# Differential attention with a feed-forward: row loads issued one pair earlier, values projected ahead of the maxima, and a reordered end

## The reference

```
q, k, v = x@Wq/2, x@Wk, x@Wv        # 32 query/key heads of width 4, 16 value heads of width 8
p       = softmax(causal(q k^T))    # for each of the 2*32 heads, 1024 x 1024
a       = (p[even heads] - lam * p[odd heads]) @ v     # lam from four small vectors
a       = a * rsqrt(mean(a^2) + eps) * rms_w * (1 - lambda_init)
x1      = layernorm(x + a @ Wo)
xr, xk  = mixes of x1 and x1 shifted by one token
out     = layernorm(x1 + sigmoid(xr@W_r^T) * (relu(xk@W_k^T)^2 @ W_v^T))
```

## Time and profile before

| | |
|---|---|
| median of 3 runs | 469.9 us (469.86 to 471.97) |
| profiled execution: its time, its span | 472.3 us, 470.6 us |
| busy: PE, DVE, ACT, POOL | 411.2, 400.3, 351.6, 224.7 us |
| mean granted clock of TensorE | 0.932 of 2.4 GHz |

### The profile page before, as it was taken

How to read it: one execution, slowest core, us unless ns; L and a number is a source line. 1 busy time by engine, 2 the same in 40 slices (tenths; PEclk the granted TensorE clock), 3 DMA queues, 4 the chain that set the end, 5 groups by cost and what they waited for, 6 DMA issues and landing times.

```text
span 470.6 us, 16533 instructions
## 1 busy us (share of the span) xinstructions
PE 411.2 (87%) x5697; PEld 193.0 (41%) x5697; DVE 400.3 (85%) x563; ACT 351.6 (75%) x734; POOL 224.7 (48%) x514
## 2 busy tenths in 40 slices
PE   5669998999998999999999999999899999999473
PEld 2235443444443443444444443444344444545352
DVE  1688898999999999999999999999999999675625
ACT  2511687888888888888888888888888888886143
POOL 7100122256554656555555555555555555557412
PEclk9855588999999999999999999999999999999777
DMA  5469311111111111111111111111111111000001
GB/s 141 166 221 329 105 48 47 48 47 49 47 49 45 45 45 45 45 45 45 45 45 45 45 45 45 45 45 45 45 45 45 45 47 47 26 3 2 22 24 45
DMA packets 21390, 28.44 MB, mean 60 GB/s; under 512 B 4960, under 2 KB 9952, under 8 KB 21232
## 3 DMA queue, kind: packets, MB, share of 16 engines
q1 hardware_dynamic: 20768, 27.58, 19.4%
q10 hardware_dynamic: 592, 0.46, 0.3%
HBM read 20.39 MB, written 9.47 MB: 63 GB/s over the span
## 4 chain that ended last, share of the span: by engine, by line
PE 36%; issue 15%; DMA 15%; DVE 12%; SPq 10%; ACT 10%; POOL 1%; ACTq 1%; DVEq 1%; POOLq 0%
DMA km<-k_rows 14%; PE acc L665 10%; PE mx L581 9%; ACT e_buf L1011 7%; DVE part_max L1112 7%; SPq L310 5%; PE ex L635 4%; SPq L296 3%; PE mx L590 2%; PE ex L692 1%; SPq L318 1%; DMA x_tok<-in_L_attn_x 1%; DVE turn_max L1125 1%; ACT max_rows L884 1%; PE mx L805 1%
## 5 line engine op out<-in xcount | busy, mean ns | idle before, releaser
L1112 DVE TENSOR_REDUCE part_max<-mx 128x2 f32<-128x1024 f32 (+2 forms) x288 | 340.5, 1214 | 27.1 <-PE mx L590 20.0
L1011 ACT ACTIVATE e_buf<-ex 128x512 f32<-128x512 f32 x576 | 304.8, 601 | 50.1 <-PE ex L635 44.7
L665 PE MATMUL acc<-e_buf,v_grp 128*32 128x256 f32 x2756 | 182.5, 354 | 7.4 <-POOL v_grp L447 2.6
L502 POOL TENSOR_SCALAR_AFFINE_SELECT e_buf<-e_buf 128x256 f32<-128x256 f32 x256 | 100.8, 412 | 166.7 <-ACT e_buf L1011 166.7
L635 PE MATMUL ex<-qe,ke 26*128 26x512 bf16 (+3 forms) x768 | 147.7, 335 | 0.7 <-ACT e_buf L1011 0.5
L581 PE MATMUL mx<-km,qm 29*128 29x128 bf16 (+3 forms) x1280 | 118.2, 272 | 19.9 <-DMA km<-k_rows 10.6
L581 PEld LDWEIGHTS mx<-km,qm 26*128 26x128 bf16 (+1 forms) x1280 | 42.3, 94 | 121.1 <-DVE part_max L1112 59.5
L665 PEld LDWEIGHTS acc<-e_buf,v_grp 128*32 128x32 f32 x2756 | 65.2, 109 | 61.7 <-issue 32.9
L635 PEld LDWEIGHTS ex<-qe,ke 26*128 26x128 bf16 x768 | 46.2, 91 | 22.4 <-ACT e_buf L1011 9.0
L485 POOL TENSOR_TENSOR r_rms<-sq_eps,minus_half 128x16 f32<-128x16 f32 x15 | 43.6, 2909 | 0.1
L590 PE MATMUL mx<-mask,pick 32*128 32x128 bf16 x512 | 26.7, 224 | 0.0
(11 more groups left out here) (137 smaller groups left out, 274.8 us busy)
## 6 DMA issues: line engine op xcount, KB each, us to landing
qm<-q_rows SPq DMA_DIRECT2D x32, 128.0 KB, 2.5
km<-k_rows SPq DMA_DIRECT2D x32, 128.0 KB, 2.6
qe<-q_rows SPq DMA_DIRECT2D x32, 128.0 KB, 2.6
ke<-k_rows SPq DMA_DIRECT2D x32, 128.0 KB, 2.7
q_rows<-part_q SPq DMA_DIRECT2D x6, 256.0 KB, 5.7
k_rows<-part_k SPq DMA_DIRECT2D x6, 256.0 KB, 5.3
q_rows<-part_q SPq DMA_DIRECT2D x6, 192.0 KB
k_rows<-part_k SPq DMA_DIRECT2D x6, 192.0 KB
```

The lines of the kernel that those rows point to most:

```text
L502: pool.affine_select(out=e, in_=e, compare_op=ALU.is_ge, fill=0.0, base=0, pattern=[[0, PAIR], [1, P]], channel_multiplier=-1)\
L665: last = pe.matmul(out, v, e, start=first, stop=over, skip_group_check=True)
L1011: nc.scalar.activation(e_buf[:, b, i, :], ex[:, ex_slot(b, i) % EX_BANKS, :], ACT.Exp).then_inc(s["exped"], 1)
L1112: nc.vector.tensor_reduce(target, mx_of(n, pr, m)[:].rearrange("p s (a b) -> p s a b", a=a), AX.X, ALU.max).then_inc(s["maxed"], 1)
```

## The change

It has four parts.

1. **SP's queue.** `load_max_rows` is issued for pair n+3 ahead of `place_maxima(n+1)`, and `load_exp_rows(n+2)` behind it. The opening loads the rows of pair 1 for the exponentials and of pair 2 for the maxima ahead of `place_maxima(0)`. The 12 writes of batch 1 go between the first pairs: 6 behind `pair(0)`, 4 behind `pair(1)`, 2 behind `pair(2)`. The fill rows of batch 1 go behind `place_maxima(0)`, and `rms_col` behind `pair(3)`.
2. **Values.** They are projected ahead of the first unit, into the `wide` banks (those of `mx`): chunks 0 and 1 after `turn_x(3)`, chunks 2 and 3 after the last q and k. DVE copies chunks 0 and 1, ACT chunks 2 and 3. Unit 0 waits for DVE's copies, unit 1 for ACT's. The body no longer waits for values.
3. **Opening, DVE and ACT.** `remainder(6)`, `low(5)`, `remainder(7)` move ahead of unit 0; `low(6)` and `low(7)` stand behind units 0 and 1. `turn_weights` moves from unit 13 to unit 4. The scaling of `wo` by the rms weights moves from the opening to the end of DVE's loop.
4. **End.** `norm_ffn` is cut into `gate_ffn` and the rest. `normalise_half(0)` goes ahead of `gate_ffn(1)`, `normalise_half(1)` and `place_half(0)` ahead of `norm_ffn(1)`, and `apply2(0)`, `apply2(1)` behind `norm_attn(3)`.

```diff
             write_parts(sp, 0, slice(HEAD, P), s["rows_b0"])
+            load_exp_rows(sp, 1, 1)
+            load_max_rows(sp, 2, 0)
+            place_maxima(sp, 0, 0, 0)
             fill_rows(1, s["rows_b1"])
-            write_parts(sp, 1, slice(0, P), s["rows_b1"])
-            sp.wait_ge(s["bounce_in"], 16)
-            sp.dma_start(rms_col[:], w_bounce.rearrange("h w -> (h w)").unsqueeze(1)).then_inc(s["rms_in"], 16)
-            place_maxima(sp, 0, 0, 0)
 
             def pair(n, pr, g):
+                if not isinstance(n, int) or n + 3 < NPAIR:
+                    load_max_rows(sp, n + 3, 1 - pr)
+                if not isinstance(n, int) or n + 1 < NPAIR:
+                    place_maxima(sp, n + 1, 1 - pr, g + pr)
                 if not isinstance(n, int) or n + 2 < NPAIR:
-                    load_max_rows(sp, n + 2, pr)
-                if not isinstance(n, int) or n + 1 < NPAIR:
-                    load_exp_rows(sp, n + 1, 1 - pr)
-                    place_maxima(sp, n + 1, 1 - pr, g + pr)
+                    load_exp_rows(sp, n + 2, pr)
...
-            group(0)
+            def write_second(part):
+                for w in range(2):
+                    write_part(sp, w, part, 1, slice(0, P), s["rows_b1"])
+
+            pair(0, 0, 0)
+            write_second(0)
             sp.wait_ge(s["rows_b0"], 16 * 2 * len(TERMS))
-            group(1)
+            pair(1, 1, 0)
+            write_second(1)
+            pair(2, 0, 1)
+            write_second(2)
+            pair(3, 1, 1)
+            sp.wait_ge(s["bounce_in"], 16)
+            sp.dma_start(rms_col[:], w_bounce.rearrange("h w -> (h w)").unsqueeze(1)).then_inc(s["rms_in"], 16)
...
-            pool.wait_ge(s["v_copied"], NCH)
+            pool.wait_ge(s["v_copied_d"], 2)
+            pool.wait_ge(s["v_copied_a"], 2)
...
-            def project_v(ch, i):
-                if i == 0:
-                    pe.wait_ge(s["wv_in"], 16)
-                    pe.wait_ge(s["rest_done"], 2 * NCH)
-                t = 4 * ch + i
-                valued = pe.matmul(narrow[ch][:, P * i:P * (i + 1)], xT[:, P * t:P * (t + 1)], wv_sb[:], start=True,
-                                   stop=True)
-                if i == 3:
-                    valued.then_inc(s["v_done"], 1)
+            def project_v(ch):
+                pe.wait_ge(s["wv_in"], 16)
+                for t in range(4 * ch, 4 * ch + 4):
+                    last = pe.matmul(wide[ch][:, P * (t % 4):P * (t % 4 + 1)], xT[:, P * t:P * (t + 1)], wv_sb[:],
+                                     start=True, stop=True)
+                last.then_inc(s["v_done"], 1)
...
             turn_x(3)
+            project_v(0)
+            project_v(1)
             for ch in (2, 3):
                 pe.wait_ge(s["xt_copied_d"], ch)
                 project_qk(2 * ch)
                 project_qk(2 * ch + 1)
+            project_v(2)
+            project_v(3)
+            pe.wait_ge(s["v_copied_d"], 2)
...
-            values = {3 + i: [(V_ORDER[i // 4], i % 4)] for i in range(12)}
-            values[NU + EARLY - 2] = [(V_ORDER[3], 0), (V_ORDER[3], 1)]
-            values[NU + EARLY - 1] = [(V_ORDER[3], 2), (V_ORDER[3], 3)]
             for u in range(NU + EARLY):
+                if u == 1:
+                    pe.wait_ge(s["v_copied_a"], 2)
                 max_unit(0, u // NU, u % NU)
-                for ch, i in values.get(u, []):
-                    project_v(ch, i)
+                if u == 4:
+                    pe.wait_ge(s["rest_done"], 2 * NCH)
+                    turn_weights()
                 if u == NU + 3:
                     turn_maxima(0, 2)
-                if u == NU + 4:
-                    turn_weights()
             pe.wait_ge(s["wt_scaled"], 1)
-            pe.wait_ge(s["v_copied"], NCH)
...
+            for ch in range(2):
+                dve.wait_ge(s["v_done"], ch + 1)
+                nc.vector.tensor_copy(value_place(ch), wide[ch].rearrange("p (k g w) -> p k g w", k=4, g=GPB))\
+                    .then_inc(s["v_copied_d"], 1)
...
+            remainder(6)
+            low(5)
+            remainder(7)
             dve.wait_ge(s["parts_set"], 3)
-            late = {0: [(remainder, 6), (low, 5)], 1: [(remainder, 7), (low, 6)], 2: [(low, 7)],
+            late = {0: [(low, 6)], 1: [(low, 7)],
                     NU: [(combine, 0, 0)], NU + 1: [(split_high, 0)], NU + 2: [(split_low, 0)]}
...
+            gate_ffn(0)
             norm_ffn(0)
             square_k(1)
-            norm_ffn(1)
             normalise_half(0)
-            apply2(0)
+            gate_ffn(1)
             normalise_half(1)
             place_half(0)
+            norm_ffn(1)
             place_half(1)
             norm_attn(2)
+            norm_attn(3)
+            apply2(0)
             apply2(1)
-            norm_attn(3)
```

More of the change, by code:

```diff
@@ L95 @@
 EX_BANKS = 3
-V_ORDER = (2, 3, 0, 1)
 def ex_slot(b, i):
@@ L896, in middle, with copy_values @@
                                rest[:, m % 4, :]).then_inc(s["mid_done"], 1)
-            def copy_values(i):
-                ch = V_ORDER[i]
-                b, kb = ch // 2, ch % 2 * 4
-                act.wait_ge(s["v_done"], i + 1)
-                src = narrow[ch].rearrange("p (k g w) -> p k g w", k=4, g=GPB)
-                dst = v_all[:].rearrange("p (b g k w) -> p b k g w", b=B, g=GPB, k=NB)[:, b, kb:kb + 4]
-                nc.scalar.copy(dst, src).then_inc(s["v_copied"], 1)
+            def copy_values(ch):
+                act.wait_ge(s["v_done"], ch + 1)
+                nc.scalar.copy(value_place(ch), wide[ch].rearrange("p (k g w) -> p k g w", k=4, g=GPB))\
+                    .then_inc(s["v_copied_a"], 1)
             act.wait_ge(s["xt_done"], 1)
             nc.scalar.copy(xT[:, 0:BANK], wide[0]).then_inc(s["xt_copied_a"], 1)
-            for b in range(B):
-                high(4 * b)
-                for m in range(4 * b + 1, 4 * b + 4):
-                    high(m)
-                    middle(m - 1)
-                middle(4 * b + 3)
-                if b == 0:
-                    for w, part in ((1, 1), (1, 2), (0, 2)):
-                        write_part(act, w, part, 0, slice(0, HEAD), s["rows_head"])
+            high(0)
+            for m in range(1, 4):
+                high(m)
+                middle(m - 1)
+            middle(3)
+            for w, part in ((1, 1), (1, 2), (0, 2)):
+                write_part(act, w, part, 0, slice(0, HEAD), s["rows_head"])
+            high(4)
+            high(5)
+            middle(4)
+            high(6)
+            middle(5)
+            high(7)
+            copy_values(2)
+            copy_values(3)
+            middle(6)
+            middle(7)
             act.wait_ge(s["lam_dots"], 2)
             nc.scalar.activation(lam_exp[:], lam_sum[:], ACT.Exp).then_inc(s["lam_exped"], 1)
-            copy_values(0)
-            copy_values(1)
-            copy_maxima(0, 2)
             act.wait_ge(s["wt_done"], 1)
@@ L1243, in square_k, with gate_ffn @@
                     .then_inc(s["k_squared"], 1)
-            def norm_ffn(ch):
+            def gate_ffn(ch):
                 dve.wait_ge(s["o_scored"], ch + 1)
@@ L1251, in norm_ffn @@
                     .then_inc(s["z_scaled"], 1)
+            def norm_ffn(ch):
                 dve.wait_ge(s["z_scaled"], ch + 1)
@@ L1294, in place_half @@
                                             ALU.mult).then_inc(s["attn_ready"], 1)
+            dve.wait_ge(s["rms_in"], 16)
+            nc.vector.tensor_scalar(rms_scaled[:], rms_col[:], (1.0 - LAMBDA_INIT) * VW ** 0.5, None, ALU.mult)\
+                .then_inc(s["rms_done"], 1)
+            dve.wait_ge(s["rms_done"], 1)
+            dve.wait_ge(s["w_in"], 16 * 4)
+            nc.vector.tensor_scalar(wo_scaled[:], wo_sb[:], rms_scaled[:], None, ALU.mult).then_inc(s["rms_done"], 1)
             norm_attn(0)
```

18 lines of the change are left out of this document (6 added, 12 removed).

## The result

The changed kernel takes **449.6 us** (median of 4 runs, 449.15 to 449.92), and the kernel before beside it 470.3 (4 runs, 469.86 to 471.97). The ratio is 0.9553, with an interval of 0.9527 to 0.9579: 20.7 us less. The forecast was 451, in 444 to 460. The profiled execution takes 449.9 us at a span of 448.2, where before it had 472.3 and 470.6.

A forecast was written before the change was run, and what follows sets the result against it. Bound: no single engine; once a pair the chain maxima copied, placed, rows issued, landed, unit 0 sets the pace. Terms 9.6 + 2.8 + 5.3 + 1.1 = 18.8 us off 472.3 give 453.5, as median 451 us; range 444 to 460.

The forecast's parts named there:

- Loop: 25 pairs of the long middle: the earlier load removes PE's wait for km, 9.6 us, 11.25 us a pair.
- I take PE's 9.9 us less the 0.3 at 101.72: Sizing of the loop's gain: PE's wait at the masked units' first matmuls, less one ahead of the 25 pairs: 9.6 us.
- DVE needs 10.99 us a pair, so at most 0.64 can be won: Loop: DVE's busy time a pair taken as limit, bounding the gain at 25 x 0.64 = 16 us.
- PE has no such reserve: Loop, at the pair's end: two transposes stand beside PE's normal work, and PE's wait moves its whole chain.
- Rival B: Loop: DVE is the only bound, 10.99 us a pair, loop gains 16 us, 444 us in all; chance 0.07.
- rival A: Loop: the wait is only half won, another wait takes a part; 6 us or less, 455 to 457; chance 0.22.
- First pairs: Three pairs from 65.20 to 101.72: 2.8 us won, including the 1.38 us wait and the lower-clock stretch.
- Placement and writes: place_maxima and exp rows behind the batch 1 writes in the first pairs: 0, with at most 2.5 us lost.
- rival C: First pairs: the writes hold up the placement, pair 2 starts 1.4 us late at a lower clock, 453.6; chance 0.14.
- Values and opening: Opening: without waits for values, unit 17 starts at 46.9 instead of 52.38; 5.3 us, within 3.8 to 5.5.
- End: Kernel's end: normalise_half(1) starts at 436.4 instead of 437.56, moving the chain behind it; 1.1 us, bounds 0.3 and 2.
- rival D: Body: TensorE's clock stays low, a pair takes 14.2 us, gain gone from 6.4 pairs on; chance 0.03 with the like.

The follow-up runs named there:

- experiment 1: Kernel before with only the change's SyncE program (wo's scaling moved with its load): 455.9 us, 0.9655.
- experiment 4: Changed kernel with load_max_rows(n+3) put back behind place_maxima(n+1), its lead of three pairs kept: 463.2 us, 0.9786.
- Experiment 3: Kernel before with only the change's order of DVE's last calls at the end: 471.0 us, 0.9961.
- experiment 10: Changed kernel with the mask matmuls of units 0 and 1 of each pair left out: 438.4 us, 0.9283.
- experiment 7: Changed kernel with turn_sums' two transposes made three times in each pair: 455.8 us, 0.9651.
- experiment 5: Changed kernel with one spare 128x256 copy on DVE in each pair: 449.7 us, 0.9519.
- experiment 9: Changed kernel with one larger spare copy (128x768) on DVE in each pair: 452.1 us, 0.9575.
- experiment 6: Kernel before with one spare 128x256 copy on DVE in each pair: 471.7 us, 0.9976.
- Experiment 12: Changed kernel with all 12 writes of batch 1 behind pair 0 instead of 6, 4 and 2: 454.0 us, 0.9619.
- experiment 2: Changed kernel with before's SyncE program and end, leaving only the values and opening of the other engines: 471.7 us, 0.9998.
- experiment 8: Changed kernel with spare transposes in TensorE's waits near the end: 446.4 us, 0.9449.

## Why the prediction was right

The forecast, its direction and its range held. Of the four terms the first pairs and the end were right in mechanism and size, the loop and the opening in mechanism with too small a size. The sum, 18.8, is below the 22.4 of the two profiled executions by the 2.9 us of the loop and the 1.4 of the opening; the end's 0.9 the other way is a matter of which execution of before was profiled.

**Loop (9.6 predicted, 12.54 measured).** The mechanism stands: experiment 1 has the whole gain from the SyncE program, and experiment 4 takes it away by putting the load back behind the placement. The step that was mis-sized is "I take PE's 9.9 us less the 0.3 at 101.72". (The 0.26 at 392.37, which belongs to the last of the 25 pairs, was left out as well.) The weight loads' idle time fell by 32.1 - 20.6 = 11.5 us, and DVE's at the masked units by 13.8 - 2.5 = 11.3. Experiment 3's trace says the same: the matmuls' wait is 11.6 us there, the weight loads' 33.8, and its 25 pairs are 14.4 us above the changed kernel's. I read it so, which no run isolates: the wait at the matmuls is only what is left of it once the weight load ahead has waited. Another 1.0 us of the 12.54 is in none of these waits. The pair fell to 11.12, not 11.25. The sentence that "DVE needs 10.99 us a pair, so at most 0.64 can be won" was no bound either: without the mask matmuls a pair took 10.75 (experiment 10).

**Which engine then sets the pace.** "PE has no such reserve" was right. 0.19 us more of PE's busy time lengthened a pair by 0.19 (experiment 7), and 0.23 less, without the mask matmuls, shortened it by 0.37 (experiment 10). DVE had 0.35 us a pair to spare (experiments 5 and 9). DVE is still a link of the chain, since a unit waits for the reduction two units back: with PE's added work 20.2 of the 20.6 us that the weight loads wait are put down to it, against 9.5 without, and a large enough addition on DVE is paid too (0.11 us of 0.46). Rival B (DVE the only bound) is excluded by the same runs, and rival A (another wait takes half) by the pair of 11.12 us.

**First pairs (2.8; 2.95).** Right: no wait, no fall of the clock. In experiments 3 and 6, with before's loads, these three pairs took 35.06 and 36.40 us, so the gain is 1.5 to 2.95.

**Placement and writes (0; 0).** Right in this order. Issue of the six writes took 4.7 us (58.15 to 62.82), not 5.6; the placement came at 65.05 and no row of PE waits for it. Experiment 12 shows that the cover is thin: 3.8 us later costs 4.4 us, by the stall and the lower clock that rival C named. By the Trainium skill, "DMA: Bandwidth & Descriptors", section "Queues, rings and completion order", which the prediction weighed, a placement is signalled only behind the earlier writes of its DMA engine. With six writes ahead no run shows a loss. With twelve there is one, but there the issue itself was late, so the run doesn't tell the two apart. The nearest rows are these: in experiment 2 PE starts 3.62 us after the placement's issue (45.69 to 49.31), and the last of twelve writes was issued 1.6 us ahead of it; in experiment 12, with 2.4 us between them, it is 2.36 us (68.86 to 71.22). The DMA engines were also busier in the first case (0.97 from 40 to 49.3 us, against 0.81 from 64 to 71.2), so this leaves it open too.

**Values and opening (5.3; 6.74).** DVE's unit 17 starts at 46.14, the forecast said 46.9. From the first unit on the count was close: 21.5 us (24.62 to 46.14) against the 21.3 of "the units are DVE's alone". The expected loss to the value tiles didn't come. The 16 matmuls of chunks 2 and 3 (20.15, 1.95 us) ran at the full clock, and PE's first unit, at 23.89, waited 1.79 us for `km`, not for them:

```profile
20.15 1.95 PE L702 MATMUL mx<-wv_sb,xT 128*128 128x128 f32 x16
23.89 0.40 PE L595 MATMUL mx<-km,qm 29*128 29x128 bf16 x8 [1.79 <-DMA km<-k_rows]
```

The prediction took the start of the opening as it was. In the trace of before two projections of q and k ran slowly, 1.91 us at 18.00 and 1.76 at 19.71; in the changed kernel all but the first take 1.02. So it is in the other traces: with the old opening (experiments 1, 3 and 6) two of the four take 1.58 to 2.08 us, and in all nine others with the first values ahead of them the first takes 1.12 or 1.13 and the rest 1.02. That the value tiles keep the clock up there is argued from this, and no run isolates it. The size was off by the 0.94 us that the first unit came sooner, and by what lies between DVE's unit 17 and the body: unit 0 in pair 0's body came 7.57 us sooner (53.67 to 46.10), and that pair then took 12.36 us instead of 11.53. Why pair 0 took longer is not settled. What I left unsaid in the sum is that the gain needs two things at once, the values out of the way and the placement ahead of the writes; each alone gives about 2 us (experiments 1 and 2), less by the traces of 3 and 6.

**Clock (rival D).** It was back some 9 us into the body (45.11 to 54.5), in the kernel before some 10 us (51.97 to 62). PE had been busy only 5.02 of the 8 us from 36 to 44, where before it was busy in all of them; the emptier opening did not delay the rise.

**End (1.1; 0.17 in these two traces, 1.0 over all).** The order did what I had worked out, to 0.03 us: 1.12 at `turn_attn(2)` here, 1.13 over nine traces. The chain behind it also ends about as much sooner, by 1.0 us on average. In the two profiled executions the lower clock hides it: chunk 3's projection took 2.05 us instead of 1.13, and `ffn_r(2)`'s matmuls 0.64 each up to 433.4, where before they ran at 0.39 but for the first. That is not the new order's doing, since experiments 1, 2 and 6 with the old order have the slow projection too. Why the clock comes back sooner in one execution than in another is not settled; experiment 8 shows only that work in the idle places keeps it up.

## What to carry to other kernels

A load that stands on a queue behind something that waits, waits with it; put it ahead of the wait, and check that what must be early (here the small placements) keeps slack behind the bulk writes. Don't take a busy share near 100% for a bound: add an operation to that engine and see whether the time follows, here 0.35 us a pair were free at 99%. In a serial end with gaps on TensorE, try filling them: that won 3.3 us here, more than the reordering of the end (about 1). Before a term of a microsecond is called lost or won, read the same stretch in a second execution: here the end alone differed by 0.8 us, and the loop with its waits by 1.8, without any change to it.

## What the runs showed of the hardware

- DVE's shown busy time is not a fixed cost. The same small cast of maxima took 308 ns on average before, 369 after and 197 in experiment 10, where the busy time of a pair fell by 0.26 us though PE's work alone was cut.
- The granted clock in an end with many short waits differs between executions of the same PE program: the eight matmuls of chunk 3's projection took 1.13 us in the trace of before, and 2.05 in experiments 1, 2 and 6.
- A group's own time is not what it adds: four more transposes a pair brought 0.43 us of their own, 0.19 us to PE's busy time and 0.19 us to the pair (experiment 7).
